# Short rows counted on ScalarE, limits and maxima on GpSimd, and reciprocals of the last mixture taken once per batch

## The reference, cut to what matters

```python
draft = jnp.einsum('bhqd,bhkd->bhqk', qr, kr)
draft = draft + jnp.where(causal_future, neg, jnp.asarray(0.0, dtype))
num_remain = max(min(Sq, MIN_REMAIN), Sq - int(Sq * MASK_OUT))
_, draft_indices = jax.lax.top_k(draft, num_remain)
...
attn = jax.nn.softmax(scores, axis=-1)
out = jnp.einsum('bhqk,bhkd->bhqd', attn, v)
...
router_logits = jnp.einsum('bsd,hd->bsh', x, Wr) + br
scores = H * jax.nn.softmax(router_logits, axis=-1)
low = jnp.einsum('bsd,hrd->bshr', x, A)
out = jnp.einsum('bshr,hor,bsh->bso', low, B, scores)
```

## Time and profile before

| what | us |
|---|---|
| median of 3 runs | 5235.53 |
| lowest and highest run | 5235.34, 5241.91 |
| the profiled execution | 5241.05 |
| its span | 5239.3 |
| busy PE, DVE, ACT, POOL | 4055.4, 3461.8, 2811.4, 41.8 |

### The profile page before, as it was taken

The page is one execution under the profiler, slowest core; times in us unless marked ns, Lnnn a source line. Parts: engine busy times, 40 slices in busy tenths (PEclk is TensorE's granted clock), DMA queues, the critical chain, the costliest instruction groups (busy, mean ns, idle before and its releaser), DMA issues. The chain is left out here.

```text
span 5239.3 us, 83348 instructions
## 1 busy us (share of the span) xinstructions
PE 4055.4 (77%) x25610; PEld 2321.0 (44%) x25752; DVE 3461.8 (66%) x10257; ACT 2811.4 (54%) x6546; POOL 41.8 (1%) x85
## 2 busy tenths in 40 slices
PE   6998999998999999546674667667667767758766
PEld 3445766665444444223442334334334434434333
DVE  3556777774333355488778888877878887874555
ACT  1115777774000011378875788788888788871000
POOL 1000000000000000000000000000000000000000
PEclk8999999999999999767876777777778777868888
DMA  4236232232111132301110111100111110103232
GB/s 144 67 75 172 53 78 65 65 85 79 48 48 48 45 73 68 64 21 26 27 23 4 27 27 23 26 14 18 26 27 26 23 26 5 26 6 93 72 73 65
DMA packets 307653, 259.69 MB, mean 50 GB/s; under 512 B 188416, under 2 KB 241936, under 8 KB 307152
## 3 DMA queue, kind: packets, MB, share of 16 engines
q1 hardware_dynamic: 306608, 253.79, 19.0%
q0 software_dynamic: 544, 0.07, 0.0%
HBM read 175.95 MB, written 77.86 MB: 48 GB/s over the span
## 5 line engine op out<-in xcount | busy, mean ns | idle before, releaser
L1063 ACT ACTIVATE a_sign<-arena,a_state 128x384 fp8e4<-128x384 f32 (+5 forms) x1056 | 917.7, 871 | 102.1 <-DVE a_state L1199 61.2
L959 PE MATMUL a_ps_s<-k,q 128*128 128x512 bf16 (+3 forms) x1474 | 463.3, 452 | 608.6 <-DVE arena L1297 404.5
L1030 ACT ACTIVATE a_probT<-a_ps_t 128x512 f32<-128x512 f32 (+3 forms) x768 | 365.7, 483 | 341.8 <-PE a_ps_t L978 262.1
L959 PEld LDWEIGHTS a_ps_s<-k,q 128*128 128x128 bf16 x1536 | 158.7, 124 | 818.9 <-DVE arena L1297 456.3
L971 PE MATMUL a_ps_t<-ident,arena 128*128 128x128 f32 x1584 | 336.1, 329 | 217.4 <-ACT a_probT L1030 182.9
L1063 ACT ACTIVATE a_sign<-a_third,a_state 128x384 fp8e4<-128x384 f32 (+2 forms) x480 | 417.3, 871 | 77.9 <-DVE a_state L1199 75.1
L737 ACT ACTIVATE a_prob<-a_x_neg,a_shift 128x640 f32<-128x640 f32 (+7 forms) x512 | 397.2, 776 | 89.2 <-DVE a_x_neg L780 63.6
L780 DVE TENSOR_SCALAR_CACHE_REDUCE a_x_neg<-a_ps_s 128x640 f32<-128x640 f32 (+7 forms) x512 | 378.8, 752 | 41.7 <-PE a_ps_s L661 26.5
L1210 DVE MAX8 a_nine<-a_below 128x8 f32<-128x256 f32 (+6 forms) x448 | 371.0, 828 | 35.2 <-issue 2.6
L676 PE MATMUL a_ps_t<-ident,a_prob 128*128 128x128 f32 x2304 | 365.6, 282 | 35.1 <-issue 12.0
L997 PE MATMUL a_ps_o<-a_probT,vals 128*64 128x128 f32 x4608 | 364.9, 300 | 0.0
(11 more groups left out here) (254 smaller groups left out, 6685.3 us busy)
## 6 DMA issues: line engine op xcount, KB each, us to landing
q<-qk SPq DMA_DIRECT2D x256, 256.0 KB, 4.5
qk<-p_qkT SPq DMA_DIRECT2D x32, 960.0 KB, 6.2
h_rows<-h SPq DMA_DIRECT2D x32, 512.0 KB, 6.8
k<-qk SPq DMA_DIRECT2D x256, 64.0 KB, 4.9
h<-tok_h SPq DMA_DIRECT2D x16, 512.0 KB, 4.0
arena<-in_wo SPq DMA_DIRECT2D x16, 512.0 KB, 10.7
o<-a_o SPq DMA_DIRECT2D x16, 512.0 KB, 2.7
q<-o SPq DMA_DIRECT2D x16, 512.0 KB, 5.6
```

The costliest lines, as they stand in the source:

```text
L959: nc.tensor.matmul(ps_s[:, n % 2, a:a + w], q[:, y, head, i * P:(i + 1) * P], k[:, y, a:a + w], start=(y == 0), stop=False, skip_group_che ...
L1030: nc.scalar.activation(probT[:, n % 4, 0:w], ps_t[:, (n + 1) % 2, 0:w], ACT.Exp).then_inc(probT_ready, 1)
L1063: ins = nc.scalar.activation(to, xs[mine][:, at:at + w], ACT.Sign, scale=-1.0, saturate=False, bias=state[:, par, 0, n:n + 1], accum_out=s ...
```

## The change

**Counting.** `count_short` is gone. ScalarE counts all 14 tiles in all five passes; `aim` of the short tiles is no longer doubled, and the scratch tile `sign` is as large as the scores. The two drains of ScalarE around the short tiles go.

**Steps of the evacuations.** The table now counts the short tiles, and `BETWEEN` is added already from step 0 (`(k + NS - 1) // NS` for `k // NS`). The evacuations of step p*14 now stand ahead of pass p's wait for `t_ready`.

**GpSimd.** A new block for GpSimd has `choose` (26 instructions in a row with 15 drains between them, on 14, 112 and 28x4 elements a partition, released by the new semaphore `ranked` at the end of pass 1) and `split_top` (7 instructions, released when all 16 tiles are fetched). `choose` raises `chosen`, for which VectorE waits in pass 2 ahead of `any_failing`; `start` no longer splits the maxima.

**Order in pass 2.** VectorE fetches the four tiles first, then waits for `chosen`, then `any_failing`, the masks, the output. `any_failing` now stands behind the wait for all turns.

**Reciprocals.** The totals of a batch (32 rows x 1024) are loaded as 128 x 256 (`compact_rows`, four DMAs), inverted by one 128x256 reciprocal, written to a new DRAM tensor `inv1`, and read by `load_inverse`, which is `load_totals` on that tensor. `scale` is a product alone. Batch 0 is inverted at the end of VectorE's slot 32, batch 1 behind `residual(0)` in the last mixture. SyncE's loop there is rewritten: output and inverse of tile j+4 are loaded when both halves of `residual(j)` are added, and the store of a tile and the load of a residual come behind it.

```diff
-                    counted = [sum(2 + i for _, i in (RANKED * EVAC_PASSES)[:k] if i > 1) + BETWEEN * (k // NS)
+                    counted = [sum(2 + i for _, i in (RANKED * EVAC_PASSES)[:k]) + BETWEEN * ((k + NS - 1) // NS)
                                for k in range(EVAC_PASSES * NS + 1)]
...
                     def count(p):
 
+                        evacs(p * NS)
                         if p == 0:
                             act.drain()
                         wait_alone(act, t_ready, s * PASSES + (p + 1), const_in, 48)
                         for n, (m, i) in enumerate(RANKED):
                             at, w = ps_seg(m, i), (i + 1) * P
-                            if n in SHORT:
-                                if n:
-                                    act.drain()
-                                evacs(p * NS + n)
-                                continue
...
-                            if n < NS - 1:
+                            if 0 < n < NS - 1:
                                 evacs(p * NS + n)
...
                     def part(p):
 
-                        if st["search"]:
-                            count_short(p)
...
                             if p == 1:
-                                choose()
-                            if p == 2:
-                                any_failing()
+                                dve.sem_inc(ranked, 1)
...
                         if p == 2:
+                            if st["score"] and not (isinstance(s, int) and s < 0):
+                                dve.wait_ge(top_ready, s + 1)
+                            for n in fetches:
+                                fetch(n)
+                            if keeps:
+                                dve.wait_ge(chosen, s)
+                                any_failing()
                             for r in keeps:
                                 mark(r).then_inc(mask_ready, 1)
                             if keeps:
                                 exact_where_needed()
                             dve.drain()
-                            for n in fetches:
-                                fetch(n)
...
+                    if isinstance(s, int) and s == PAIRS:
+                        dve.wait_ge(inverted, LOADED)
+                        nc.vector.reciprocal(compact[:, :], compact[:, :]).then_inc(inverted, 1)
...
-                for j in range(NT):
-                    sp.wait_ge(y_ready, j + 1)
-                    sp.dma_start(out_dram[j * P:(j + 1) * P, :], y[:, j % 2, :]).then_inc(y_out[j % 2], 16)
+                for j in range(NT + 2):
+                    if j + RING == TT:
+                        sp.wait_ge(inverted, LOADED + 1 + 16 * 4)
                     if j + RING < NT:
+                        sp.wait_ge(added, 2 * j + 2)
                         load_o(j + RING)
-                        load_h(j + RING)
+                    if j == 0:
+                        sp.wait_ge(inverted, LOADED + 1)
+                        compact_rows(sp, 1, compact, inv_dram, inverted, False)
+                    if j >= 2:
+                        sp.wait_ge(y_ready, j - 1)
+                        sp.dma_start(out_dram[(j - 2) * P:(j - 1) * P, :], y[:, j % 2, :]).then_inc(y_out[j % 2], 16)
+                        if j - 2 + RING < NT:
+                            load_h(j - 2 + RING)
```

203 lines of the change are left out of this document (113 added, 90 removed).

## The result

The changed kernel takes 5341.53 us (5340.75 to 5343.11, four runs), the kernel before 5237.11 (5235.34 to 5241.91, four runs): 1.020 times as long, 95% interval 1.018 to 1.022. It is 104 us slower. The forecast of 5280 had the sign and its range held the time, but the loss is two and a half times the 39 us that the sum gave, and the time lies outside the 5250 to 5310 that the prediction called its forecast. Of the profiled executions the spans are 5339.5 and 5239.3, 100.2 apart.

The account below looks back on a forecast made before the run. No engine was held full: a chain carried by ScalarE bounds the attention, one of stores, loads and a reciprocal the last mixture. 5241.05 + 175 (slots) + 1 (slot 32) - 137.4 (last mixture) = 5280 us, range 5222 to 5350.

Parts of the forecast that it names:

- that of the slots: Second attention, slots 2 to 31: each takes 84.1 us instead of 78.3, +5.8, so +175 over thirty slots.
- Evacuations: Passes 0 and 1 of a slot: evacuations ahead of the signs move the start of pass 2 from 39.4 to 44.9, +5.5.
- Signs: ScalarE in the attention: two more tiles of 256 columns and one drain less lengthen each pass by 0.87 us.
- Slots 0 and 1, slot 32: Ends of the attention: slots 0 and 1 together taken as 0, slot 32 +1 us for the failing rows.
- GpSimd.: `choose` in the attention slot: starts at 36.7, takes 8 us (2.6 to 14.2) of 14 available, hidden.
- The rival of two colliding engines: Attention: `choose` beside VectorE's `narrow` of pass 1 costs 0.6 to 2.4 us a slot; 5316 at 1.2; chance 0.15.
- The rival of a raised clock: Attention: TensorE keeps 2.4 GHz, a slot takes 79, total 5135 to 5174; chance 0.13 together with free evacuation places.
- Late GpSimd: Attention: `choose` takes 17.5 us, 3.3 too long, +100, total 5380; chance 0.10.
- loads bound the mixture: Last mixture: loads stay the bound, say 23 us a tile, +60, total 5340; chance 0.08.
- Last mixture: Last mixture: first product 5.2 us earlier, product 2 3.2, 13 tiles at 18.4 save 127, last product 2; sum -137.4.
- the signs to look for: Expected in the trace, among others: ScalarE's waits for TensorE double; VectorE waits over 3 us in passes 0, 1 and 3.

Follow-up runs that it names:

- e2: The changed kernel with the evacuations and their table of steps back at the old places: 5141.6 us.
- e7: The changed kernel with two and three added TensorE products, results overwritten, ahead of turns 11 and 12: 5269.6 us.
- e10: The changed kernel with GpSimd's chain of 26 instructions run twice before it raises `chosen`: 5474.7 us.
- e4: The changed kernel with 9 added TensorE products ahead of the scores of tile 14 and 11 ahead of turn 2, results overwritten: 5290.2 us.
- e8: The changed kernel with the added products of both e4 and e7: 5222.0 us.

## Why the prediction was wrong in size, and what of it held

The sign and the main mechanism, evacuations ahead of the signs that come back only in part, were right (e2). The term that failed is that of the slots, put at +5.8 us each, +175 in all; it measured +7.9 each, +236. The step in it is *Evacuations*, up to the start of pass 2: said +5.5, measured +8.0 (46.2 for 38.3). That the range of 5222 to 5350 held the time is in part luck: it reached over 5310 for the sake of two engines colliding and of loads that bound the mixture, and neither came about.

*Signs*, +0.87 a pass: right, slightly less, 0.75 to 0.81 in passes 2 to 4. Passes 2 to 4 and the slot's end came to 38.8 (39.2 forecast, 38.9 before); a pass of 14 signs took 11.4.

*Evacuations*, the step that failed. The prediction's list gave pass 2 at 44.9. In the 11 slots without a second fall of the clock this is about what the trace has (44.7 in the slot at 3566.26). It was wrong in two things:

- It held the clock to have one rise in a slot, because the earlier trace rows show one. It listed the gaps that the new order makes (TensorE waiting for evacuation 10) and gave them a length only. They made the clock fall again in 19 of 30 slots, 2.7 us each (30.85 less 28.15): 51 us. e7 shows that the gaps bring it: with them filled it goes, and 72 us with it; in slot 31, where they are not filled, it stays.
- It took one slot of before as the base, the one of the earlier trace rows with 78.3, pass 1 at 22.6 and pass 2 at 39.4. The 29 slots without exact selection have 77.19 on the mean: in most the clock rises earlier than in that one. 1.1 us in 30 slots are 33 us.

Together 84 us; against it stand 0.45 by which pass 1 began earlier in the undisturbed slots than forecast (28.15 for 28.6) and 0.4 at the slot's end (38.8 for 39.2), 25 us. 175 + 84 - 25 is 234, and 236 were measured.

*Slots 0 and 1, slot 32*: right, 0 and, with the start of the mixture, -4.8 for -4.2.

*GpSimd.* `choose` was forecast from 36.7, 8 us long, hidden. Timelines of GpSimd (its first and last instruction) and of VectorE in the slot at 3566.26:

```profile
3602.95 0.21 POOL L1095 TENSOR_SCALAR a_equal<-a_over 128x14 f32<-128x14 f32 x1 [39.22 <-DVEq L1271]
...
3612.00 0.20 POOL L1134 TENSOR_TENSOR a_code<-a_marked 128x1 f32<-128x1 f32 x1
```

```profile
3608.69 0.17 DVE L1225 TENSOR_TENSOR a_state<-a_state,search 128x14 f32<-128x14 f32 x1 [5.93 <-ACT a_sign L1065]
...
3610.62 0.25 DVE L1251 COPY_PREDICATED a_state<-a_open,a_new 128x14 f32<-128x14 int32 x1
...
3613.33 0.21 DVE L1275 STREAM_TRANSPOSE a_codeT<-a_code 128x32 f32<-128x32 f32 x1
...
3624.37 0.18 DVE L1251 COPY_PREDICATED a_state<-a_open,a_new 128x14 f32<-128x14 int32 x1
```

It starts at 36.7 and takes 9.25. VectorE asks at 47.1, 1.1 after it is done, and doesn't wait. The forecast gave the choice 14 us from its start and 8 for its length, so 6 to spare. The trace has 13.1: VectorE has 6.4 us of work behind the wait and must be done by 56.2, when the signs of pass 2 are. With a length of 9.25 that leaves 3.8 to spare, and e10 bears it out. The 0.25 for a drain had no row; here two instructions on 14 elements with a drain between them start 0.36 to 0.38 apart, and 0.15 to 0.18 without one.

*The rival of two colliding engines* is out. `choose` does run beside `narrow` of pass 1, from 3608.69 to 3610.87, 2.18 against 2.08 in pass 2; the 0.1 is a predicated copy of 0.25 instead of 0.18 and 0.03 in another. By the rule of the Trainium skill ("SBUF — State Buffer", "Who interferes with whom") a VectorE instruction with two inputs in SBUF contends with a GpSimd instruction that reads SBUF, and the one that comes second is blocked for the whole of the other. The trace doesn't bear this out: the products, sums and differences of two tensors kept their lengths within 0.01, GpSimd's instructions beside them took 0.20 to 0.22 as elsewhere, and all of `narrow` grew by 0.1.

*The rival of a raised clock* was right in its mechanism (79 a slot where the clock was up from the start and stayed up, e4 and e8) and wrong about this kernel: by the windows of 2 us the clock is up in the first 8 us of none of its 30 slots. *Late GpSimd* and *loads bound the mixture* didn't come about: see e10 and the tile of 18.4.

*Last mixture*, -137.4: the product terms came to -131.1 for -132.2, and the start to -4.8 with slot 32. Of its parts product 2 was 2 us later than said (44.3 for 42.3), waiting for the last of the first loads.

Of the signs to look for, two were wrong: ScalarE's wait for TensorE's turns rose by 46% (262 to 383 us), not to twice, and VectorE's waits for signs were 8.2, 5.9, 2.8 and 2.1 (in the slot at 3566.26), so over 3 in passes 0 and 1 only. And one of GpSimd's 26 instructions took 0.61, over the 0.5 that was named as a sign against the prediction; it did no harm, as the whole chain took 9.25.
